# Node attention: query projection and head matrix multiplied once on the chip, residual added by a second product in the output projection

## The reference

```python
for c in range(6):
    q = ew[c, 0] * (nodes[c - 1] @ We[eq] + be[eq])
    k = ew[c, 1] * (nodes[snode] @ We[ek] + be[ek])
    v = ew[c, 2] * (nodes[snode + nsrc // 2] @ We[ev] + be[ev])
    o = mha(q, k, v, Wq[c], Wk[c], Wv[c], Wo[c])   # 8 heads of 16; qh = q @ Wq[c], and so on
    nodes[c] = act_w[c] * o + q
out = layernorm(nodes[5])
```

## Time and profile before

| | |
|---|---|
| median of 3 runs | 2217.35 us (2217.06 to 2220.44) |
| the profiled execution, its own time | 2223.95 us |
| its span, first to last instruction | 2221.9 us |
| mean granted TensorE clock | 0.949 |
| busy, share of the span: PE, PEld, DVE, ACT, POOL | 92%, 38%, 78%, 67%, 15% |

### The profile page before, as it was taken

The page is one execution under the profiler, slowest core; times in us unless marked ns, Lnnn a source line. Parts: engine busy times, 40 slices in busy tenths (PEclk is TensorE's granted clock), DMA queues, the critical chain, the costliest instruction groups (busy, mean ns, idle before and its releaser), DMA issues.

```text
span 2221.9 us, 32029 instructions
## 1 busy us (share of the span) xinstructions
PE 2039.9 (92%) x10812; PEld 846.9 (38%) x10812; DVE 1737.5 (78%) x3501; ACT 1486.8 (67%) x2004; POOL 341.7 (15%) x385
## 2 busy tenths in 40 slices
PE   5748886999999999999999999999999999999995
PEld 2224443333333333444444444444444444443332
DVE  5856887788787877888888888888878888888884
ACT  4743453566666677777777777777777777776664
POOL 1101332000000011111111111111111111113223
PEclk9977786799999999999999999999999999999998
DMA  3001104233333355566566656556666566665630
GB/s 103 19 24 54 56 33 86 43 66 75 63 75 67 82 104 107 117 109 109 109 109 109 108 109 109 108 110 109 109 110 108 108 109 109 109 108 101 98 58 25
DMA packets 137197, 195.63 MB, mean 88 GB/s; under 512 B 20152, under 2 KB 55632, under 8 KB 137040
## 3 DMA queue, kind: packets, MB, share of 16 engines
q1 hardware_dynamic: 137040, 193.63, 45.5%
HBM read 75.45 MB, written 23.73 MB: 45 GB/s over the span
## 4 chain that ended last, share of the span: by engine, by line
PE 81%; DVE 13%; issue 4%; ACT 1%; POOL 1%; DMA 1%; DVEq 0%; POOLq 0%; SPq 0%; ACTq 0%
PE bank_s L1031 27%; PE bank_o L1069 22%; PE bank_x L1054 6%; DVE nm L1386 5%; PE bank_m L1082 3%; PE bank_x L1017 3%; PE bank_x L996 3%; PE bank_x L1004 2%; PE bank_m L1102 2%; PE bank_x L983 2%; PE bank_x L1128 2%; PE bank_s L934 1%; DVE big L1275 1%; PE bank_m L1092 1%; PE bank_m L1041 1%
## 5 line engine op out<-in xcount | busy, mean ns | idle before, releaser
L1386 DVE TENSOR_REDUCE nm<-bank_s 128x1 f32<-128x512 f32 x2048 | 1336.2, 685 | 342.3 <-PE bank_s L1031 341.4
L821 ACT ACTIVATE big<-bank_x 128x1024 f32<-128x1024 f32 x1024 | 1048.0, 1024 | 486.5 <-PE bank_x L1054 458.9
L1031 PE MATMUL bank_s<-kst,qst 62*128 62x512 f32 x2048 | 837.5, 469 | 53.1 <-DVE nm L1386 52.5
L1054 PE MATMUL bank_x<-qst,kst 64*128 64x512 f32 x2048 | 750.0, 447 | 1.6 <-ACT big L821 1.6
L1031 PEld LDWEIGHTS bank_s<-kst,qst 62*128 62x128 f32 x2048 | 358.9, 187 | 693.3 <-DVE nm L1386 609.4
L1069 PE MATMUL bank_o<-big,at 128*32 128x512 f32 x4096 | 556.4, 616 | 2.2 <-ACT big L821 2.0
L1054 PEld LDWEIGHTS bank_x<-qst,kst 64*128 64x128 f32 x2048 | 304.3, 187 | 10.2 <-issue 6.0
L605 POOL CAST at<-at 128x512 fp32r<-128x512 f32 x112 | 68.2, 609 | 1273.3 <-ACT at L752 1035.8
L607 POOL TENSOR_TENSOR at<-at 128x512 fp32r<-128x512 f32 x112 | 143.3, 1280 | 10.0
L1069 PEld LDWEIGHTS bank_o<-big,at 128*32 128x32 f32 x4096 | 81.2, 108 | 153.1 <-issue 149.2
L829 ACT ACTIVATE big<-bank_x,big 128x128 f32<-128x128 f32 x256 | 68.7, 376 | 27.3 <-issue 11.6
(11 more groups left out here) (154 smaller groups left out, 1511.4 us busy)
## 6 DMA issues: line engine op xcount, KB each, us to landing
at<-nodes_d SPq DMA_DIRECT2D x144, 256.0 KB, 5.9
kst<-at SPq DMA_DIRECT2D x288, 128.0 KB
qst<-at SPq DMA_DIRECT2D x288, 128.0 KB
nodes_d<-big SPq DMA_DIRECT2D x48, 256.0 KB, 3.1
at<-w_d SPq DMA_DIRECT2D x48, 193.0 KB, 5.8
at<-x2T_d SPq DMA_DIRECT2D x32, 256.0 KB, 4.4
kst<-at SPq DMA_DIRECT2D x128, 64.0 KB
qst<-at SPq DMA_DIRECT2D x128, 64.0 KB
```

What stands on the lines that cost most here:

```text
L821: act.activation(PT[:, kp, h, :, :], ring.take()[0].rearrange("p (c n) -> p c n", c=2), ACT.Exp, scale=x.c.scale).then_inc(S["c_ex"], 1)
L1031: pe.matmul(bank_s[:, n % 2, :], qst[rows, x.r, h, t * P:(t + 1) * P], kst[rows, x.r, h, :], start=True, stop=True).then_inc(S["c_s_ps"], 1)
L1054: mm = pe.matmul(sec(to, j), kst[rows, x.r, h, kc_ * P:(kc_ + 1) * P], qst[rows, x.r, h, :], start=True, stop=True)
L1386: dve.tensor_reduce(nm[:, k, at_n:at_n + 1], bank_s[:, n % 2, :], AX.X, ALU.max, negate=True).then_inc(S["c_red"], 1)
```

## The change

The product of the edge weight and the head matrix of the queries is formed once for each node in the preparation (`q_product`, with its bias `b_product(c, 0)`), so that `proj_q`, `ev_qT`, their semaphores and the ring q_sb are gone and `proj_qh` reads the node's input directly, from one of six tiles nq. The key projection moves from (1,6) to (1,2), the query head product from (1,7) to (1,6), and (1,7) is left with `turn_x3` of the first layer only. `out_proj` gets a product ahead of the one it had: edge weight times node input, accumulated in bank_m, which is the residual. Its bias column now holds both biases. The output is no longer formed by `node_out` on VectorE but by `ev_wo` on ScalarE, a copy with bias, after the exponential of step (1,0). The rows of w_d are the same 643 columns in all; 128 of them move from the transfer of `load_qk` to that of `load_o`, and the packed input weights grow by 6 x 64 KB. `load_qk` now waits for the evictions (c_kf_ev, c_qf_ev) in place of the products, and for the output projection that used the nq tile before.

```diff
-PK = ["WeQ", "WqP", "WeKT", "WkP", "WeVT", "Wv", "Wo"]
+PK = ["WeQ", "WeQT", "WqP", "WeKT", "WkP", "WeVT", "Wv", "Wo"]
-WA = 3 * P + 2
-WN = WA + 2 * P + 1
+WA = 2 * P + 2
+WN = WA + 3 * P + 1
+NQ = 6
...
-                when((S["c_kh_ps"], x.u - 1), *[(S["c_qh_ps"], x.un - 1)] * x.c.node)
+                when((S["c_kf_ev"], x.u - 1), *[(S["c_qf_ev"], x.un - 1), (S["c_wo_ps"], x.un - NQ + 1)] * x.c.node)
...
-                    sp.dma_start(t[:, WA:WA + L], row(nodes_d, x.un)).then_inc(done, 16)
-                    sp.dma_start(t[:, WA + L:WA + 2 * L], row(nodes_d, (x.un // 40) * NB + x.un % NB)).then_inc(done, 16)
+                    sp.dma_start(t[:, WA:WA + L], row(nodes_d, (x.un // 40) * NB + x.un % NB)).then_inc(done, 16)
+                    sp.dma_start(nq[x.un % NQ], row(nodes_d, x.un)).then_inc(done, 16)
...
-                act.activation(qf, ring.take()[0][:, 0:L], ACT.Copy).then_inc(S["c_qf_ev"], 1)
+                act.activation(qf, ring.take()[0][:, 0:L], ACT.Identity, bias=st_qk[x.half][:, 2 * P:2 * P + 1]).then_inc(S["c_qf_ev"], 1)
...
+            def ev_wo(x):
...
+                need(act, S["c_wo_ps"], x.un + 1)
...
+                act.activation(no_sb, bank_m[:, :], ACT.Identity, bias=st_o[x.half][:, 2 * P:2 * P + 1]).then_inc(S["c_wo_ev"], 1)
...
+                pe.matmul(q_product(c), wv(c, "WeQT"), wv(c, "WqP"), start=True, stop=True)
+                pe.matmul(b_product(c, 0), wv(c, "WqP"), vec(c, 0), start=True, stop=True)
...
                 misc(S["c_wo_ev"], x.un + 1)
-                pe.matmul(bank_m[:, :], st_o[x.half][:, 0:P], ctxT, start=True, stop=True).then_inc(S["c_wo_ps"], 1)
+                pe.matmul(bank_m[:, :], st_o[x.half][:, P:2 * P], nq[x.un % NQ], start=True, stop=False)
+                pe.matmul(bank_m[:, :], st_o[x.half][:, 0:P], ctxT, start=False, stop=True).then_inc(S["c_wo_ps"], 1)
...
                             if i == 2:
-                                proj_q(ahead)
-                                proj_kh(only(ahead, False))
+                                proj_kh(ahead)
                             if i == 6:
-                                proj_kh(only(ahead, True))
+                                proj_qh(ahead)
                             if i == 7:
-                                proj_qh(ahead)
                                 turn_x3(last)
...
-                        if (k, i) == (1, 0):
-                            node_out(last)
```

More of the change, by code:

```diff
@@ L734, in _ @@
             ring = Slots()
[L736 to L742, removed]
             def ev_kh(x, src=None):
@@ L880, in body @@
                         else:
+                            if i == 0:
+                                ev_wo(last)
                             if i == 1:
@@ L883, in body @@
                             if i == 2:
-                                ev_qT(ahead)
-                                ev_kh(only(ahead, False))
+                                ev_kh(ahead)
                             if i == 6:
-                                ev_kh(only(ahead, True))
+                                ev_qh(ahead)
                             if i == 7:
-                                ev_qh(ahead)
                                 ev_x3T(last)
@@ L894, in _ @@
             ev_cT(end)
+            ev_wo(end)
             ev_final(end)
@@ L973, in slot @@
                 return to
-            def proj_q(x):
-                x = only(x, True)
-                if x is None:
-                    return
-                t = st_qk[x.half]
-                need(pe, S[f"c_qk{x.half}"], loaded(x, kn.loads_qk))
-                to = slot(S["c_q_ev"], x.un + 1)
-                pe.matmul(to[:, 0:L], t[:, 0:P], t[:, WA:WA + L], start=True, stop=True).then_inc(S["c_qT_ps"], 1)
             def proj_kh(x, to=None):
@@ L1001, in proj_qh @@
                     return
[L1002 removed]
+                need(pe, S[f"c_qk{x.half}"], loaded(x, kn.loads_qk))
                 to = slot(S["c_qf_ev"], x.un + 1)
[L1004 removed]
+                pe.matmul(to[:, 0:L], st_qk[x.half][:, 0:P], nq[x.un % NQ], start=True, stop=True).then_inc(S["c_qh_ps"], 1)
             def value(x, to=None):
@@ L1375, in _ @@
             dve.wait_ge(S["p_mm"], 2)
-            dve.tensor_copy(po_sb[:, :, WN - 1], bank_o[:, 0:NODES]).then_inc(S["p_ev"], 1)
+            for c in range(NODES):
+                i = dve.scalar_tensor_tensor(po_sb[:, c, WN - 1:WN], vec(c, 0), vec(c, 3), bank_o[:, c:c + 1], ALU.mult, ALU.add)
+            i.then_inc(S["p_ev"], 1)
             def reduce(x, k, n):
@@ L1505, in divide @@
                                   rec.unsqueeze(3).broadcast_to([P, NT, GH, x.c.hd]), ALU.mult).then_inc(S["c_ot_ev"], 1)
-            def node_out(x):
-                x = only(x, True)
-                if x is None:
-                    return
-                need(dve, S["c_wo_ps"], x.un + 1)
-                if final(x):
-                    need(dve, S["f_tT_ps"], final(x))
-                else:
-                    need(dve, S["c_store"], 16 * (NB + x.un))
-                dve.scalar_tensor_tensor(no_sb, bank_m[:, :], st_o[x.half][:, P:P + 1], q_sb[x.r], ALU.add, ALU.add).then_inc(S["c_wo_ev"], 1)
             def residual(x, step):
@@ L1608, in _ @@
             final_norm(last, 3)
-            node_out(end)
             for step in range(4):
```

43 lines of the change are left out of this document (25 added, 18 removed).

## The result

The changed kernel takes 2250.78 us (2249.43 to 2255.98, four runs), the kernel before 2218.89 us (2217.06 to 2222.44, four runs): ratio 1.0147, 95% interval 1.0128 to 1.0165. Slower, as forecast, and within the range, though the median had been put at 2242.7. The profiled execution took 2249.84 us with a span of 2247.8, against 2249.3 forecast for it.

What follows compares the result with a forecast made beforehand. TensorE was taken to bound the node units, its instructions standing one behind another. 40.4 - 17.6 + 1.7 + 0.8 = +25.3 us takes the median 2217.35 to 2242.7; range 2229 to 2256 for 8 in 10.

Steps and rivals of the forecast that it cites:

- The product at (0,7): Second output projection product at (0,7): 0.86 us a unit with nothing to absorb it, 47 times, 40.4 us (upper bound 48.4).
- What (1,7) gives back: Query product gone from (1,7): 0.42 us won in 42 units, 17.6 us, because VectorE's reductions are next in line.
- Rival 1: (1,7) gives back all, TensorE alone holding the next unit: 41 to 46 us won, time 2217 +- 5; chance 0.12.
- rival 3: Nothing comes back: reductions, bank_x's slot at (0,0) or bank_m's new reader hold TensorE; 2260; chance 0.12.
- VectorE to ScalarE: Output formed at (1,0) on ScalarE, taking 0.74 us a unit off VectorE: zero effect, upper bound 4.7 us.
- rival 2: VectorE paces the unit, so 0.74 us less at (1,0) shortens it: 2185; chance 0.07 with the smaller gains.
- Units 14 and 16, and the transfers: Gain at (1,7) at most 1.03 each against GpSimd's split up to 1.0: zero within 2 us; transfers zero.
- The preparation: Twelve more weight products still end ahead of VectorE's start; VectorE's added evictions and column operations cost 0.8 us, at most 1.6.
- The last output projection: Stands alone on an idle TensorE, two passes took 1.71 us; two more add up to 1.7 us.
- The last node: Units 57 to 60, VectorE also doing the final norms: nothing won at (1,7); the added product priced as elsewhere, 0.86 us.
- The starting point: Profiled execution 2223.95 us, 6.6 over the median 2217.35; the sum +25.3 was added to both, giving 2249.3 and 2242.7.

Runs made afterwards that it cites:

- no_residual: The changed kernel without the residual product, so its output projection is one product again; 2207.82 us, ratio 0.9948 to the kernel before.
- slot_only: The changed kernel passing over one slot of bank_x at (1,7), with no product added; 2268.23 us, ratio 1.0218 to the kernel before.
- dve_out: The changed kernel with the node's output formed on VectorE again at (1,0), not on ScalarE; 2250.53 us, ratio 1.014 to the kernel before.
- split: The changed kernel with residual product at (1,6), context product at (1,7), query product at (0,7), last node unchanged; 2218.94 us, ratio 0.9999 to the kernel before.
- split3: split2 with the last node's residual product at its own (1,7) in a bank_x slot, added by VectorE; 2206.21 us, ratio 0.9942 to the kernel before.
- before_again: The kernel before, unedited, run again for a second profile; 2219.21 us, ratio 1.0003 to the kernel before.
- split2: split with the query product at (0,6) and the transpose of the context at (0,7); 2219.96 us, ratio 1.0001 to the kernel before.
- filled17: The changed kernel with one more product into bank_m at (1,7), its result unread; 2259.06 us, ratio 1.0178 to the kernel before.
- slot17: The changed kernel with one more, unread product at (1,7) in a slot of bank_x; 2266.79 us, ratio 1.0207 to the kernel before.
- gap12: The changed kernel with key projection back at (1,6) and query product at (1,7), leaving (1,2) empty; 2251.87 us, ratio 1.0148 to the kernel before.

## Why the prediction was right

- **The product at (0,7).** 0.86 us, worked out from four products in a row, is what the timeline shows (1.89 against 1.03) and what no_residual takes off each unit. Its whole cost fell on the path.
- **What (1,7) gives back.** 0.42 was forecast; it is 0.38 in the timeline and from no_residual (27.70 - 27.32). Rival 1 (all of it, 1.03) and rival 3 (nothing) are both out. The reason given, that VectorE's reductions are next in line, is right for the changed kernel and was half of the story for the kernel before: there the exponential and the slot held the step, not TensorE's own product. Size and sign came out because the sum went from the measured times of the very place to the reductions. That the slot goes with the product was no part of the working, and that is luck: slot_only, with the product gone and its slot still passed over, takes the 3.69 us of the kernel before, so that nothing would have come back.
- **VectorE to ScalarE.** Zero, as forecast; dve_out shows it and rules rival 2 out. By that rival's reading (the Trainium skill, Perfetto Trace Analysis, § Identifying the Most-Contended Engine) VectorE was to be relieved first, TensorE being judged by its weight loads; here relieving VectorE of 0.7 us a unit moved nothing, and 0.86 us a unit taken off TensorE moved 43 us.
- **Units 14 and 16, and the transfers.** In units 14 and 16 (1,7) falls from 2.69 to 1.94; (1,4) and (1,5) rise from 1.93 + 2.01 to 2.65 + 2.22 in unit 14 and by as much in unit 16. The gain and GpSimd's split cancel to 0.2 us a unit, as forecast. Nothing in the steady part waits for a transfer.
- **One sentence was wrong.** "The residual product could run while the context is transposed and evicted": it could not, for until that eviction bank_m holds the transposed context itself. It took a place in another step (split) or a slot of bank_x (split3).
- **The preparation** was forecast at 0.8 us. By the timelines the weight products take 8.2 us in place of 5.5 and still end, at 157.36, ahead of VectorE's start on them at 157.99; from there to VectorE's first operation behind them it is 14.14 us, against 13.38 before.
- **The last output projection** was forecast at 1.7 more for itself. Its rows, and the eviction behind it:

```profile
2227.77 1.88 PE L1102 MATMUL bank_m<-at 128*128 128x512 f32 x2 [0.78 <-ACT big L792]
...
2229.44 1.91 PE L1103 MATMUL bank_m<-big,at 128*128 128x512 f32 x2
...
2231.39 0.69 ACT L804 ACTIVATE big<-bank_m,at 128x512 f32<-128x512 f32 x1 [3.77 <-PE bank_m L1103]
```

  From 2227.77 to 2231.35 the four passes take 3.58 us, 1.87 more than the 1.71 of two. The granted clock averages 0.52 over these four passes and 0.60 over the two of the kernel before, against 1.00 in the steady part.
- **The last node** was taken at 0.86 a unit, 5.2 us for six, and cost 6.3 to 7.2. The product itself is 0.7 a unit there; the rest lies in the two units that have a stretch at half clock, which the forecast did not have.
- **The starting point.** The sum was +25.3 and the profiled executions differ by 25.9. The medians differ by 31.9: before's profiled execution lay above its median by 6.6, after's did not. Against before_again the same table gives 32.4, of which 18.8 are units 17 to 57, 7.2 the last node, 1.7 the end and 4.7 lie ahead of unit 17. The last is within what two profiles of one and the same kernel differ there (5.9 us), and no run separates it. The forecast of the median, 2242.7, was 8.1 low, within its range: 6.6 for this, and 1.5 because the median of three that it started from, 2217.35, is 2218.89 with the fourth run.

## What to carry to other kernels

In a pipeline whose steps are ordered by hand, the number of products says little: the same work took 28.18 and 27.31 us a unit, depending on which step a product stood in and whether it took a slot of bank_x: 0.86 at (0,7) behind another one, 0.20 at (1,7) in bank_m, 0.38 at (1,7) in a slot. Price a removed piece by what the next engine holds from that moment, and by the buffer slot it took; the slot alone can be worth more than the work. An empty step is worth something only where the engine whose work was taken out was the limit, and its gain is partly paid back in the step behind it; where another engine is the limit it is the place to put work for nothing.

## What the runs showed of the hardware

TensorE at half clock in the last node. Two windows of the changed kernel there, and one of the kernel before:

```profile
2036.00:2038.50 2.50, 1.43 (x5) 0.61 (x4) 2.50 (x5) 1.87 (x3) 2.36 (x3) 1.00 0.00 0
2040.50:2043.00 2.50, 2.50 (x16) 0.70 (x12) 1.25 (x3) 0.82 (x1) 1.20 (x1) 0.50 0.65 143
```

```profile
2143.00:2146.00 3.00, 3.00 (x14) 0.87 (x13) 1.54 (x3) 1.02 (x1) 0.00 (x0) 0.50 0.03 5
```

and the rows between and in the first two:

```profile
2038.57 0.50 PE L1031 MATMUL bank_s<-kst,qst 62*128 62x512 f32 x1 [0.87 <-DVE nm L1387]
...
2042.08 1.81 PE L1069 MATMUL bank_o<-big,at 128*32 128x512 f32 x8
```

TensorE was busy 1.43 of 2.50 us and stood idle 0.87 us for VectorE up to 2038.57; 1.6 us later, at 2040.2, the granted clock falls to 0.50, that is 1.2 GHz, and eight passes that take 1.06 us at 1402.95 take 1.81. By the records of the granted clock such stretches last 3.4 to 6.8 us. Ahead of the last 60 us of the program, the changed kernel has three in the last node, the kernel before one in either profile, slot_only four; no_residual, dve_out and split2 three, split two; filled17, slot17 and gap12, with a product at (1,7), one, and split3 none. But the same idle time stands ahead of units 59 and 60 of the changed kernel (0.85 us at 2071.34, 0.87 at 2102.97), and no stretch follows:

```profile
2071.34 0.49 PE L1031 MATMUL bank_s<-kst,qst 62*128 62x512 f32 x1 [0.85 <-DVE nm L1387]
```

What a stretch goes with can be read by unit. Of units 58 to 60, those without one take 31.6 to 31.8 us in the changed kernel, dve_out, slot_only, split and split2 and 30.9 in no_residual, those with one 32.7 to 32.9 and 32.3: 1.1 to 1.4 us more. So the idle time of an empty step can cost more than itself. No run forced or kept off a stretch by itself; that it is the cause rests on which units have it.

VectorE and GpSimd side by side. Ahead of the wait at 2038.57 two small operations of VectorE are drawn out, in the changed kernel:

```profile
2035.27 1.27 POOL L666 TENSOR_TENSOR big<-big,lngb 128x512 f32<-128x512 f32 x1 [1.38 <-DVE big L1274]
...
2035.70 0.86 DVE L1483 CAST mp<-nm 128x16 fp32r<-128x16 f32 x1
...
2036.62 1.27 POOL L668 TENSOR_TENSOR big<-big 128x512 f32<-128x512 f32 x1
...
2037.08 0.84 DVE L1486 TENSOR_TENSOR mp<-nm,mp 128x16 fp32r<-128x16 f32 x1
```

They take 0.86 and 0.84 us, and 0.17 each in the middle of the run; either one ends within 0.03 us of the GpSimd operation beside it (2036.54 and 2037.89). The kernel before has the same at this step of units 57 to 61 (0.86 and 0.83). It is a part of what makes VectorE the limit there.
